# TensorE's completion signals moved from the last matmul of a group to a drain behind it

## The reference

```python
h = jnp.maximum(_layernorm(x, axis=-1), 0.0)
x = x + _L0_gnn_ref(h, edge_index, ...)          # two rounds: sum of h[src] over dst, then a small MLP
x = x + _L1_gnn_ref(h, edge_attr3_2x32, src, dst, ...)   # attention over the edges of a node
x = x + _L2_gnn_ref(h, edge_attr_2, weight, edge_index)  # 4x4 tent basis, sum over src
x = x + _L3_gnn_ref(h, edge_index, edge_attr_3, ...)     # spline convolutions, 125 weight matrices, sum over src
```

## Time and profile before

| what | us |
|---|---|
| median of 3 runs | 11856.13 |
| lowest and highest run | 11834.23, 11860.02 |
| the profiled execution, its own time | 11889.0 |
| its span, first to last instruction | 11887.2 |

### The profile page before, as it was taken

How to read it: one execution, slowest core, us unless ns; L and a number is a source line. 1 busy time by engine, 2 the same in 40 slices (tenths; PEclk the granted TensorE clock), 3 DMA queues, 4 the chain that set the end, 5 groups by cost and what they waited for, 6 DMA issues and landing times. The chain is left out here.

```text
span 11887.2 us, 143975 instructions
## 1 busy us (share of the span) xinstructions
PE 5759.6 (48%) x32326; PEld 4601.4 (39%) x32455; DVE 6368.5 (54%) x16774; ACT 3373.4 (28%) x7561; POOL 6278.5 (53%) x8257
## 2 busy tenths in 40 slices
PE   4232233434556666466666466666433333742222
PEld 2111133333434344355555466666233333422222
DVE  6444555554411111466656788888455555645555
ACT  0000022222133333111111577777311112321111
POOL 3777566664155555455555344444155555046665
PEclk8555555655566666566666555555655555865555
DMA  6331222211555555222223799999211111776666
GB/s 192 111 111 57 60 56 58 57 55 51 189 184 192 178 192 188 43 68 67 68 64 65 278 349 350 349 350 346 76 38 37 37 38 36 285 260 206 196 204 182
DMA packets 895764, 1760.16 MB, mean 148 GB/s; under 512 B 488178, under 2 KB 488487, under 8 KB 891096
## 3 DMA queue, kind: packets, MB, share of 16 engines
q0 software_dynamic: 317952, 1023.05, 26.8%
q1 hardware_dynamic: 538584, 598.40, 15.0%
q10 hardware_dynamic: 39168, 138.04, 2.9%
HBM read 1150.49 MB, written 611.50 MB: 148 GB/s over the span
## 5 line engine op out<-in xcount | busy, mean ns | idle before, releaser
L1771 POOL DMA_INDIRECT got<-corners,now x1664 | 1606.8, 966 | 1812.6 <-DVE now L1757 768.7
L1771 POOL DMA_INDIRECT got<-node_rows,now x1664 | 1607.3, 966 | 1689.4 <-issue 1327.2
L1771 POOL DMA_INDIRECT got<-patches,now x832 | 794.1, 954 | 906.2 <-issue 625.0
L948 POOL DMA_INDIRECT d_rows<-row x832 | 834.8, 1003 | 545.8 <-issue 534.6
L1677 PE MATMUL made_p<-weights,turned 64*128 64x320 f32 x2450 | 792.7, 639 | 564.9 <-ACT z L1701 297.9
L2574 PE MATMUL sum_p<-msg_s,hot_s 128*128 128x64 f32 x3328 | 737.2, 423 | 597.0 <-DVE msg_s L2029 597.0
L699 POOL DMA_INDIRECT s_rows<-row_now,pos_i x784 | 758.0, 967 | 373.7 <-issue 363.5
L2574 PEld LDWEIGHTS sum_p<-msg_s,hot_s 128*128 128x128 f32 x3328 | 717.6, 332 | 605.9 <-DVE msg_s L2029 605.9
L2113 PE MATMUL acc_p<-msg,hot_s 128*128 128x32 f32 x1664 | 376.2, 402 | 984.8 <-DVE msg L2037 808.0
L1819 DVE TENSOR_TENSOR a<-a,sum_p 128x64 f32 x832 | 183.6, 221 | 1246.4 <-remote 727.1
L1701 ACT COPY z<-made_p 128x384 f32<-128x384 f32 x1225 | 525.4, 489 | 976.5 <-DMA d_rows<-row 471.2
(11 more groups left out here) (423 smaller groups left out, 15024.2 us busy)
## 6 DMA issues: line engine op xcount, KB each, us to landing
corners<-z SPq DMA_DIRECT2D x245, 960.0 KB
corners<-z SPq DMA_DIRECT2D x98, 864.0 KB
d_rows<-empty ACTq DMA_DIRECT2D x32, 1586.0 KB
row<-d_rows SPq DMA_DIRECT2D x104, 488.0 KB
corners<-z SPq DMA_DIRECT2D x49, 672.0 KB
s_rows<-empty ACTq DMA_DIRECT2D x32, 962.0 KB
row<-s_rows SPq DMA_DIRECT2D x104, 296.0 KB
got<-node_rows,now POOLq DMA_INDIRECT x1664
```

Source lines behind the costliest of these rows:

```text
L948: pool.indirect_dma_start(out=d_rows, out_offset=bass.IndirectOffsetOnAxis(ap=to[:, t, DPOS:DPOS + 1], axis=0), in_=row[b][:, t, :], in_of ...
L1771: pool.indirect_dma_start(out=to[b][:, t, :], out_offset=None, in_=table, in_offset=bass.IndirectOffsetOnAxis(ap=indices.now[b][:, t:t + 1 ...
```

## The change

At nine places the semaphore is no longer added to by the last matmul of a group, but by a drain instruction of PE behind it. In the turn this holds for all three signals of a group and for the opening one, in the tent for all three, in the sort, the second sum's sums and the last gather for the one. The order of the instructions, the waits and the counts stay as they are; per run 98 + 1 + 3 x 104 + 104 + 3 x 104 + 104 = 931 drains are added.

```diff
@@ place_phase
                             m = nc.tensor.matmul(upon(1, first, T + 1 - first), k.ones16[:], mid(one[:, u, :], T + 1 - first),
                                                  start=False, stop=u == T - 1)
-                        m.then_inc(ranked, 1)
+                        pe.drain().then_inc(ranked, 1)
@@ turn_phase
                 for n in range(2):
                     m = nc.tensor.matmul(sum_p[1][:, n, :], k.zero16[:], zeros(k), start=True, stop=True)
-                m.then_inc(summed, 1)
+                pe.drain().then_inc(summed, 1)
...
-                        m.then_inc(turned, 1)
+                        pe.drain().then_inc(turned, 1)
...
-                        m.then_inc(picked, 1)
+                        pe.drain().then_inc(picked, 1)
...
-                        m.then_inc(summed, 1)
+                        pe.drain().then_inc(summed, 1)
```

## The result

The changed kernel took 11879 us (median of 20 runs, 11856 to 11911), the kernel before beside it 11855 us (20 runs, 11831 to 11887). The ratio is 1.0024, 95% interval 1.0015 to 1.0032: 24 us longer, where 876 us less had been forecast. The profiled execution took 11901.9 us.

A forecast was written before the change was run, and what follows sets the result against it. POOL's issuing was taken as the floor, with late PE signals making it stop. 11889.0 - 971 + 50 (second sum) + 47 (drains) = 11015 us profiled, 10980 us as median; range 10700 to 11300, outer range 10500 to 12100.

The forecast's parts named there:

- The floor: POOL's unpaused issuing of transfers and fillers: 1056 us in the sort, 1121 in the turn, 1101 in each gathering phase.
- the late signals: PE's semaphore signals reach ACT and DVE microseconds late while POOL issues transfers back to back; stretches 157 to 456 us longer.
- a busy way out for the increments that PE's matmuls carry: Five phases: matmul increments leave PE in order, each held up for itself; a drain's increment would go another way.
- the 971 us: Gain from prompt signals in sort, turn, tent and last gather: nine tenths of the 1079 us their bounds add up to.
- the sort's last drain: Drain at the sort's end in the trace of before, ending 9.5 us late; spoke loudly against the change.
- the pending increment: End of the sort: the last matmul's increment, still pending in PE, held the drain; with nothing pending a drain is prompt.
- both readings of the drain: Sort's end: held by a pending increment, or the matmul itself counts as unfinished so long; 900 us apart.
- the pending `made`: Second sum: the table multiplications' signal stays on the matmul; if held, the drain waits for it. No gain expected, +50 us.
- half falls into waits that exist: Second sum: multiplications behind the drain lose 457 us at most, about 200 if half coincides with existing waits.
- The drain's own price: All 931 drains: some 0.05 us each behind the matmul, 47 us if all lies on the path.
- the first two: Rivals, drain as late as signal: nothing else happens, 11856 us, chance 0.09; or PE stands still, 12100 us, chance 0.28.
- the rival had 200: Rival that PE stands still for a late drain: second sum about 200 us, turn at most 110; 12100 us, chance 0.28.
- the first rival: Drain as late as the signal, every wait stays, drains lie in PE's idle time: 11856 us, give or take 24; chance 0.09.

The follow-up runs named there:

- the bare drains' run: Kernel before, signals left on the last matmuls, 930 drains carrying nothing added behind them, where completions are late: 11729.6 us beside 11669.9, ratio 1.0055.

## Why the prediction was wrong

**The floor and the late signals: right.** POOL's floor and what is above it held: with nothing late the stretches came to within 5 us of the forecast in the sort and the last gather, 25 us below it in the tent, 39 above it in the turn. The kernel before is 2000 us faster on such a chip. I had counted only the five phases; the attention's scores, which aren't touched, fall as well, from 1663 to 1179 us.

**The step that failed** is the reading "a busy way out for the increments that PE's matmuls carry", and with it the 971 us. I took it from the two signals of a group that left singly. That they leave one by one only says that they leave in order; completions that are late and come in order look the same, and in the bare drains' run a signal and its drain too come some 0.7 or 1.4 us apart when not together. The row that could have told, the sort's last drain, was read rightly as "the matmul itself counts as unfinished for so long", and then set aside for the pending increment. With the bare drains both come out together, to 0.01 us in 31 of 46 held groups of the turn, and the drains with nothing pending are held as long: 2965 us of holds in the recorded profile. Nine tenths of 1079 us should have been nothing. That 11879 us lies inside the outer range of 10500 to 12100 is no success: it was that wide because it took in both readings of the drain.

On this the Trainium skill was nearer than I was: page PSUM — Partial Sum Buffer, section Engine vs sequencer instructions, says that a drain waits until the engine is fully idle and that the increment belongs on the matmul. Where completions are prompt the traces agree: the drains end 0.02 us behind the last matmul. The recorded profile, 30.19 us of drain with 3.67 us of matmuls left to do, agrees only if the matmuls count as unfinished for so long. The Trainium skill's other figure, some 26 ns for an increment (page TensorE: Matmul & The Clock Gate, section The cost: per-tile semaphore tail), no run here prices by itself; it has no room for holds of 37 us.

**The second sum: the size was right, the reason only in part.** I forecast +50 us and it grew by 50.4. That close it is luck: the same old code's stretch scattered by 16 to 20 us between profiles of one chip, and where the drain stood there alone it was 51 to 71. I had put the hold down to the pending `made`; in the sort and the tent drains are held with nothing pending, so the completion of the sums themselves is enough for it, though in this phase the two aren't told apart. That the multiplications queue behind the drain was the mechanism, and "half falls into waits that exist" was too careful: of 239 us more standing a fifth to a third came through.

**The drain's own price: too high.** 931 times 0.05 us, 47 us in the sum. With nothing late a drain that carries the signal ends 0.02 us behind the matmul, 20 us in all 930 (a bare one 0.05 us, as the prediction read it), and none of it lies on the path: 1.0000 (0.9991 to 1.0009) in the time.

**The rivals.** What happened lies between the first two. The drain is as late as the signal (both had that), and PE stands still for it: +50 in the second sum where the rival had 200, +26 in the turn where it had at most 110. Against that stands the gain in the last gather, which no rival had. Without it the five stretches would have grown by 75 us, 0.6%. That the time came within the first rival's 11856 give or take 24 us is therefore two effects that cancel, and not that rival's mechanism. To a drain as late as the signal I had given 0.09 and 0.28 together, to a prompt one 0.63.

**The clock.** I expected no change that counts. In the second sum the granted clock fell from 0.67 to 0.63 of full speed, and on one chip from 0.68 without to 0.64 with the drain there; PE moves between its two levels, 1.2 and 2.4 GHz, and stood idle for longer before the multiplications, 527.9 us in 144 times where it had been 266.0 in 141. A weight load of line 1677 took 286 ns in the mean instead of 260. It goes with the standing still, and I haven't priced it by itself.

## What to carry to other kernels

Before moving a signal, ask whether it is the message or the completion that is late, and let a bare drain behind the signal tell you: if both come out together, a drain as the carrier won't help, it only adds standing still, which costs where independent work is queued behind it and little where PE waits next anyway. When TensorE's completions are late while POOL issues transfers back to back, look at POOL's pitch, not at TensorE: 4% slower issuing, with all the drains in the kernel, gained 2.3%. But measure on more than one chip, for the same filler (with one phase's drain) cost 1.9% where completions were prompt.

## What the hardware showed that I had not expected

- The same kernel took 9884 to 9888 us on some chips and 11670 to 11887 us on others. The message phase (transfers in runs of eight, with pauses) takes 1756 to 1758 us on all of them, the other six phases with POOL's indirect transfers take longer on the second kind. Unbroken issuing isn't enough: in the turn of the whole change, on a chip with prompt completions, POOL issued for 1169 us without a pause of over 0.8 us, and no drain was held. Why chips differ isn't known.
- TensorE's completions (increments and drains alike) came up to 39 us late (37 in the recorded profile), while its next matmuls could start on time. They were prompt when the same bytes were moved by direct transfers of SP, at 354 GB/s.
- The hold grows with how long POOL has been issuing without a pause: in the last gather of the recorded profile a median of 0.02 us up to 9 us into a stretch, 2.2 at 9 to 12, 5.2 at 12 to 16, 22.8 at 16 to 25. It isn't a rule for every phase: in the second sum of the same profile the median is 6.0 us for the 54 drains whose sums ended 3 to 6 us into a stretch.
- Making PE wait for its own signal ahead of the next group in the last gather made the kernel 0.6% faster (0.9940) where completions are late.
